# Attention 0 of a two-layer adaLN kernel: side operations two slots apart, a gated output projection in token-major form, and five elementwise steps moved to GpSimd

## The reference

```
mod = (silu(L0_c) @ L0_wmod).reshape(16, 6, 1, 128);  sa, ca, ga = mod[:, 0], mod[:, 1], mod[:, 2]
ga = sign(ga) * max(|ga|, 0.25)
h = layernorm(x) * (1 + ca) + sa
q = h @ Wq + bq;  latent = h @ Wl + bl;  k = latent @ Wk + bk;  v = latent @ Wv + bv     # 16 heads of 8
out = softmax(q k^T / sqrt(8)) v
x = x + ga * (out @ Wo + bo)
```

## Time and profile before

| | us |
|---|---|
| median of three runs | 950.3 |
| lowest and highest | 946.4, 954.19 |
| the profiled execution, its own time | 953.58 |
| its span, first to last instruction | 951.8 |
| attention 0 within the span | about 21 to 348 |

### The profile page before, as it was taken

How to read it: one execution, slowest core, us unless ns; L and a number is a source line. 1 busy time by engine, 2 the same in 40 slices (tenths; PEclk the granted TensorE clock), 3 DMA queues, 4 the chain that set the end, 5 groups by cost and what they waited for, 6 DMA issues and landing times. The chain is left out here.

```text
span 951.8 us, 18404 instructions
## 1 busy us (share of the span) xinstructions
PE 775.1 (81%) x6066; PEld 577.7 (61%) x6066; DVE 677.0 (71%) x1680; ACT 604.3 (63%) x1365; POOL 283.5 (30%) x359
## 2 busy tenths in 40 slices
PE   3458888888688864799999993799988884999996
PEld 3213444444344343799999992678777763888884
DVE  3165777778478627577777654789999964898885
ACT  0214777777477745688888873467877762556553
POOL 3441223242221000000000002234544431767674
PEclk9999999999799976899999996799999995999998
DMA  4353443425953000000000000000000051346340
GB/s 130 41 57 40 56 48 50 54 44 57 171 93 48 4 1 2 1 1 1 1 1 1 2 1 1 1 1 2 2 1 2 1 142 42 89 112 180 107 111 23
DMA packets 76159, 41.04 MB, mean 43 GB/s; under 512 B 6712, under 2 KB 74144, under 8 KB 76064
## 3 DMA queue, kind: packets, MB, share of 16 engines
q1 hardware_dynamic: 76064, 39.83, 22.5%
HBM read 24.62 MB, written 2.23 MB: 28 GB/s over the span
## 5 line engine op out<-in xcount | busy, mean ns | idle before, releaser
L563 DVE TENSOR_REDUCE att_negmax<-att_p_max 128x2 f32<-128x512 f32 x256 | 165.0, 686 | 87.5 <-PE att_p_max L443 86.4
L647 ACT ACTIVATE att_probs<-att_p_sT 128x1024 f32<-128x1024 f32 x128 | 129.6, 1022 | 58.6 <-PE att_p_sT L449 57.6
L443 PE MATMUL att_p_max<-att0p_QK 48*128 48x256 bf16 x512 | 93.8, 295 | 35.9 <-DVE att_negmax L563 11.7
L2050 POOL TENSOR_TENSOR moe_z_lo<-moe_z,moe_z_hi 128x512 fp32r<-128x512 f32 x64 | 96.8, 1528 | 58.2 <-ACT moe_z_hi L2003 56.4
L449 PE MATMUL att_p_sT<-att0p_QK 51*128 51x256 bf16 x512 | 87.6, 284 | 1.2 <-DMA att0p_QK<-att_maxT 1.2
L443 PEld LDWEIGHTS att_p_max<-att0p_QK 48*128 48x128 bf16 x512 | 34.1, 98 | 86.8 <-DVE att_negmax L563 46.2
L928 PE MATMUL ffn0s_p_h<-ffn0s_u_hi,ffn_h_hi 128*128 128x256 f32 x256 | 69.3, 306 | 13.6 <-DVE ffn0s_u_lo L1193 13.0
L472 PE MATMUL att_p_o<-att_probs,att0p_V 128*32 128x256 f32 x1024 | 72.0, 401 | 8.9 <-ACT att_probs L647 7.8
L2041 DVE TENSOR_TENSOR moe_z<-moe_act_u,top_raw 128x512 f32<-128x512 f32 x64 | 73.6, 1150 | 2.2
L1193 DVE TENSOR_TENSOR ffn0s_g_lo<-ffn0s_g,ffn0s_g_hi 128x512 fp32r<-128x512 f32 x64 | 43.3, 691 | 38.8 <-ACT ffn0s_g_hi L1138 37.3
L1134 ACT ACTIVATE ffn0s_g<-ffn0s_p_h,top_ffn_scales 128x256 f32<-128x256 f32 x128 | 54.9, 489 | 19.5 <-PE ffn0s_p_h L929 19.3
(11 more groups left out here) (289 smaller groups left out, 2295.0 us busy)
## 6 DMA issues: line engine op xcount, KB each, us to landing
top_raw<-combine SPq DMA_DIRECT2D x32, 512.0 KB, 6.6
att0p_QK<-att_parts SPq DMA_DIRECT2D x192, 64.0 KB
top_X<-in_L_attn_x SPq DMA_DIRECT2D x4, 512.0 KB, 7.0
top_raw<-in_L_ffn_h_w SPq DMA_DIRECT2D x2, 1024.0 KB
out_x<-top_X SPq DMA_DIRECT2D x8, 256.0 KB, 2.3
prep_wmod<-in_L_wmod SPq DMA_DIRECT2D x2, 384.0 KB, 3.5
top_raw<-in_L_ffn_w_w SPq DMA_DIRECT2D x3, 256.0 KB
att0p_QK<-att_maxT SPq DMA_DIRECT2D x32, 12.0 KB
```

What stands on the lines that cost most here:

```text
L443: mm = pe.matmul(p_max[u % 2][:, i, :], QK[r][rows, g, 0, i * P:(i + 1) * P], QK[r][rows, g, 1, :], start=True, stop=True)
L563: dve.tensor_reduce(negmax[:, :, w, g], p_max[u % 2][:], AX.X, ALU.max, negate=True).then_inc(maxed, 1)
L647: act.activation(probs[g % 2][:, t % 2], p_sT[t % 2][:], ACT.Exp).then_inc(exped, 1)
L2050: pool.tensor_tensor(z_lo[e % RING][:], z[e % RING][:], z_hi[e % RING][:].bitcast(F32), ALU.subtract).then_inc(z_lo_ready, 1)
```

## The change

In `attention0`:

- The side operations of TensorE stand at even slots only, two apart: out 0, ln 2, max_turn 4, O0 6, qk 8, v 10, O1 12, back 14. Each now stands ahead of its slot's tiles.
- The scores of a batch begin at slot 8 of step n-3, not at slot 6 (`SHIFT`). pv stands behind the tiles of slots 14, 0, 4 and 8, not of 11, 15, 3 and 7.
- The projection is token-major: `OTn` is the stationary operand, and the moving one is a copy of Wo whose columns are already multiplied by the gate of that batch. The gated bias is added by a second matmul with one row of ones. `act_y`, `pe_turn_y` and their buffer are gone. The projection and the addition to x move to slot 0 of the next step, so the pipeline is one step longer (21 steps).
- The gated copies of Wo (`wo0_all`, 16 x 128x128) need the gates along the free axis. They are written element by element to DRAM (128x16 values) and read back broadcast to all partitions (1 MB), on SyncE, ahead of the first stack. GpSimd multiplies them by Wo, one batch a step (`pool_wo`).
- Part 0 of the q and k split and the four operations on the maxima move to GpSimd. `negmax` has two buffers. In a step GpSimd now does maxima, parts, layer norm, gated Wo in this order; before it was layer norm, parts.
- VectorE's layer-norm statistics move from slot 2 to slots 8 and 10.

```diff
+SHIFT = 8
+PES = {"out": 0, "ln": 2, "max_turn": 4, "O0": 6, "qk": 8, "v": 10, "O1": 12, "back": 14}
+PV_AT = {14: (3, 0), 0: (4, 1), 4: (4, 2), 8: (4, 3)}
+DVE = {"add": 0, "O0": 6, "stats": 8, "aggr": 10, "O1": 12}
+ACTS = {"hT": 2, "maxT": 4, "qk": 8, "v": 10, "OTn": 14}
+OT_AT = {0: 0, 2: 1, 6: 2, 10: 3}
...
         def pe_out(pe, b):
             pe.wait_ge(OTn_ready, b + 1)
-            pe.matmul(p_m[:, 0:S], k.wo0[:], OTn[:], start=True, stop=True).then_inc(y_made, 1)
+            pe.wait_ge(wo_ready, b + 1)
             for i in range(NT):
+                out = p_m[:, i * D:(i + 1) * D]
+                pe.matmul(out, OTn[:, i * P:(i + 1) * P], k.wo0_all[:, b, :], start=True, stop=False)
+                mm = pe.matmul(out, k.ones_row[0:1, :], k.gbo0_row[0:1, b, :], start=False, stop=True)
+            mm.then_inc(y_made, 1)
...
         def act_qk(act, b, r):
...
-            act.wait_ge(qk_ready, b + 1)
-            at_least(act, stacked, 16 * STACK_DMAS * (b - 1))
-            act.activation(parts[r % 2][:, :, 0], qk[:], ACT.Copy).then_inc(part0_ready, 1)
...
         def pool_parts(pool, b, r):
+            pool.wait_ge(qk_ready, b + 1)
+            at_least(pool, stacked, 16 * STACK_DMAS * (b - 1))
+            pool.tensor_copy(parts[r % 2][:, :, 0], qk[:]).then_inc(part0_ready, 1)
...
+        def pool_wo(pool, b):
+            if b == 0:
+                pool.wait_ge(k.ga0_loaded, 16)
+            pool.tensor_tensor(k.gbo0_row[:, b, :], k.wo0_all[0:1, b, :], k.bo0_row[:], ALU.mult).then_inc(gbo_ready, 1)
+            pool.wait_ge(gbo_ready, b + 1)
+            pool.tensor_tensor(k.wo0_all[:, b, :], k.wo0_all[:, b, :], k.wo0[:], ALU.mult).then_inc(wo_ready, 1)
...
         def pool_step(pool, n, r):
+            if batch_valid(n - 3):
+                pool_negmax(pool, n - 3)
+            if batch_valid(n):
+                pool_parts(pool, n, r)
             if batch_valid(n + 1):
                 pool_normalise(pool, n + 1)
-            pool_parts(pool, n, r)
+            if batch_valid(n - 2):
+                pool_wo(pool, n - 2)
...
-        LAST = B + 4
+        LAST = B + 5
...
         @block.sync
         def _(sp):
+            sp.dma_start(k.ga0_dram.rearrange("b d -> d b"), k.mod[:, 0, GA, :], allow_slow_non_contiguous=True
+                         ).then_inc(k.ga0_stored, 16)
+            sp.wait_ge(k.ga0_stored, 16)
+            sp.dma_start(k.wo0_all[:], k.ga0_dram.rearrange("(o b) d -> o b d", o=1).to_broadcast([P, B, D])
+                         ).then_inc(k.ga0_loaded, 16)
```

More of the change, by code:

```diff
@@ L42 @@
 SROWS = MAXROW + 3
-PES = {"ln": 0, "max_turn": 2, "qk": 3, "O0": 5, "v": 8, "O1": 9, "back": 11, "out": 12, "turn_y": 14,
-       "pv_s": (11, 15), "pv_t": (3, 7)}
-DVE = {"negmax": 0, "stats": 2, "O0": 6, "O1": 10, "add": 15}
-ACTS = {"hT": 0, "maxT": 1, "qk": 3, "v": 7, "OTn": 11, "y": 12, "OT_s": (11, 15), "OT_t": (3, 6)}
+SHIFT = 8
[4 more added lines that the diff above has]
+OT_AT = {0: 0, 2: 1, 6: 2, 10: 3}
 F = 512
@@ L345, in attention0 @@
         parts = [sb(f"parts{n}", [P, 2, 3, S], BF16) for n in range(2)]
-        negmax = sb("negmax", [P, NT, 2, PAIRS])
+        negmax = [sb(f"negmax{n}", [P, NT, 2, PAIRS]) for n in range(2)]
         negrest = sb("negrest", [P, NT, 2, PAIRS])
@@ L455, in pe_max_turn @@
             pe.wait_ge(neg_ready, b + 1)
[L456 to L459 removed]
+            if b + 3 < B:
+                pe.wait_ge(hT_ready, b + 4)
+            at_least(pe, x_added, b - 1)
             for i in range(NT):
@@ L509, in pe_step @@
                     pe_max_turn(pe, s)
+                if slot == PES["O0"] and batch_valid(t):
+                    pe_turn_O(pe, t, 0)
                 if slot == PES["qk"] and batch_valid(f):
@@ L599, in dve_step @@
         def dve_step(dve, n, r):
-            f, m, s, t = n, n - 2, n - 3, n - 4
+            f, m, s, t, y = n, n - 2, n - 3, n - 4, n - 5
             for slot in range(TILES):
-                if slot == DVE["negmax"] and batch_valid(s):
-                    dve_negmax(dve, s)
+                if slot == DVE["add"] and batch_valid(y):
+                    dve_add(dve, y)
                 if slot == DVE["O0"] and batch_valid(t):
@@ L657, in act_OTn @@
             act.activation(OTn[:], p_m[:, 0:S], ACT.Copy).then_inc(OTn_ready, 1)
-        def act_y(act, b):
-            act.wait_ge(y_made, b + 1)
-            at_least(act, y_turned, b)
-            act.activation(yT[:], p_m[:, 0:S], ACT.Identity, bias=k.gbo0[:, bass.ds(b, 1)],
-                           scale=k.mod[:, 0, GA, bass.ds(b, 1)]).then_inc(yT_ready, 1)
         def act_step(act, n, r):
             f, m, s, t = n, n - 2, n - 3, n - 4
-            for slot in range(TILES):
+            for slot in range(0, TILES, 2):
+                if slot in OT_AT and batch_valid(t):
+                    act_OT(act, t, OT_AT[slot])
                 if slot == ACTS["hT"] and batch_valid(f):
@@ L781, in _ @@
                     pool_step(pool, turn * NB + (WHOLE.start + r), r)
-            for n in range(WHOLE.stop, B):
+            for n in range(WHOLE.stop, B + 3):
                 pool_step(pool, n, n % NB)
```

139 lines of the change are left out of this document (62 added, 77 removed).

## The result

The changed kernel takes **991.6 us** (median of four runs, 983.7 to 995.75), the kernel before on the same chip 952.2 (946.4 to 954.19): a ratio of 1.0414, 95% interval 1.033 to 1.0499. It is slower by 4%. The forecast, 961, was slower by 1%, with a chance of 0.43 for more than 1% slower and 0.46 for equal within 1%; the measured time lies above the range, which ended at 973.

What follows compares the result with a forecast made beforehand. No engine is full; the chain of handovers between three engines sets the step. Whole steps -2, stacks +2, gates +5, late loads +2, end +5 sum to +12 on 953.6, moved onto the median: 961 us, range 942 to 973.

Steps and rivals of the forecast that it cites:

- the chain: Handovers between engines from pv group 0 to the next, said to set the whole step: 16.5 us against 16.67.
- the late loads: Step 13, maxima behind four weight loads: loads issued 4.8 us into the step, maxima needed 6.0 later, was 8.1; +2 us.
- One sign: Expected in the trace of whole steps: in each, pv group 1 waiting for the copy to OT0.
- The end: Steps 16 to 18 and the extra step, by the chain walk less 5%: +5 us, bounds +1 and +8.
- The projection: Token-major projection on TensorE beside the chain after pv group 0: eight instructions at v's rate, 1.28 us, ready at 2.84.
- the other branch: Exponential 3, then the copy to OT0 and its handover: lets pv group 1 start 2.82 us behind group 0.
- The whole steps: Whole steps 16.5 us against 16.67, nearly nothing: -2 us over 12 steps, bounds -6 to +6.
- the stacks: Stack DMAs ahead of the next maxima: need 18.4 us, have 17.6; 0.15 a step, +2 us, bounds 0 and +5.
- The gates: Gates' store and 1 MB load ahead of the first stack on SyncE: it lands 0 to 9 us later; +5 taken.
- A: Rival: chain looser than walked, whole step about 15.4 us, 945 us in all, or 938; chance 0.22.
- B: Rival: stack misses slot 8 every step, TensorE waits 0.8 us there, steps of 17.4, 970 us; chance 0.2.

Runs made afterwards that it cites:

- Experiment 1: Changed kernel with the four groups of products with V behind the odd tile, one tile later: 956.2 us, ratio 1.0003 to the kernel before.
- experiment 4: Changed kernel with four more score products, read by nobody, in every slot of steps 18 and 19: 980.3 us, ratio 1.0252 to the kernel before.
- experiment 2: Changed kernel without the ones-row product that adds the gated bias: 977.8 us, ratio 1.0192 to the kernel before.
- experiment 9: Changed kernel with products with V behind the odd tile and without the ones-row bias product: 950.8 us, ratio 0.9951 to the kernel before.
- experiment 10: Kernel before with only the moves to GpSimd (part 0 of the split, four operations on the maxima): 948.9 us, ratio 0.9956.
- experiment 3: Changed kernel with the gates' store behind stack 0 and their load behind stack 1: 988.4 us, ratio 1.0326 to the kernel before.

## Why the prediction was wrong

**What was right.** The prediction named the products with V ahead of the odd tile as what costs, and walked the chain: it gave gaps of 2.82, 4.18, 4.08 and 5.42 between the groups, and the trace has 3.32, 4.18, 4.18 and 5.41. It said that the maxima turn would wait for the layer-norm scale (it stood for 0.75 and started at 161.22; that scale ended at 161.12, GpSimd's last part of the maxima at 158.01), that GpSimd would not be full (7.5 us of 17.08) nor be waited for, and +2 for the late loads (+2.2). Experiment 1 shows that the place of the products is the cause of nearly the whole loss. One sign did not hold: group 1 waited for the projection, 3.32 behind group 0, and not for the copy to OT0.

**The end, +5 and bounds of +1 to +8: the step that failed.** It measured +21.7, and this term alone puts the time above the range. The term priced every product at the full clock and added to before's four intervals what the walk of the chain gave, which makes 14.9, 14.8, 14.3 and 12.2. Measured were 19.25, 15.97, 18.85 and 18.90. The 16.8 that it is short have four parts. The clock: in steps 18 and 19 TensorE's products are on the chain and run at 1.2 GHz, and the two steps pay 6.8 for it, as experiment 4 shows. The walk itself: with the clock held up these two are 16.69 and 14.29, so it was short by 2.4 and 2.1. Step 16, 4.4 over, where TensorE waited 2.62 for the DMA of the turned maxima behind four late loads and its clock fell to 0.66 at 320 to 325 us; how those 4.4 divide was not measured. In experiment 2 the same step had a wait of 1.23 there, kept the full clock and took 15.96. The last 1.2 are in step 17. Nothing in the argument had asked what thinner work does to the clock, though the trace before already shows 0.70 at 345 to 350 us. With the products one tile later the four intervals are 56.8, next to the 56.2 of the forecast; that is luck, since the term was walked for a schedule that this kernel does not have. Its scaling is also a little off: 5% off 15.4 and 15.0 are 14.6 and 14.3, where it took 14.8 and 14.3.

**The projection, 1.28 of TensorE.** It measured 1.66 (155.92 to 157.58). The term priced its eight instructions as v's four, 0.16 each, and they take 0.21. The projection was called an equal of the other branch at 2.84, so its 0.4 over went straight to the step. Experiment 2 took the ones rows out and got 0.40 a step.

**The whole steps, -2, and the stacks, +2.** Together 0 was forecast and +4.1 came. Against the forecast, which had the place of the products in it, the bias product is all of it: without it the step is 16.68. The forecast counted 12 whole steps where there are ten, which is 0.3 us of its sum. The stacks cost nothing in the changed kernel's whole steps, where no wait stands at slot 8; the wait appears when the step is shorter (experiments 1, 9). So +2 was too much here, and it hid part of the miss.

**The gates, +5.** +2.8, within a scatter of 4. The parts were off in opposite senses. Alone, the 2064 packets took 9.3% of 16 engines for 10 us, 7 ns each and not 44 to 70, and had moved by 23.3 us; but the landing was seen at 31.7, at the late end of the 28 to 32 that the term gave. By the Trainium skill's rule (DMA: Bandwidth & Descriptors, Specifications), that transfers under 512 bytes are read, modified and written back, the term should have been nearer +7; no slower packet is to be seen in this store. The DMA view of 21 to 31 us of the changed kernel:

```profile
q1 hardware_dynamic: 2064, 0.01, 9.3%
...
gates<-top_mod SPq DMA_DIRECT2D x1, 8.0 KB, 10.9
```

**The rivals.** A's step of 15.4 is nearly what the changed kernel does with the products one tile later, but in every second step only (15.56), and even then the time only equals that of before, since start, late loads and end give the gain back. A's sum was also off: by the prediction's own terms the others are +14 and not +10, so 949 and not 945. B's wait at slot 8 exists and was hidden. No run takes the two slots and the gated projection apart, so what each of them does alone stays open.

**Where the change's gain went.** Of its three ideas, the moves to GpSimd bring 0.64 a step and 0.44% alone. Two slots and the gated projection together, with the products in the better place, bring 0.1 to 0.2 a step more (15.93 on average over ten whole steps in experiment 1 against 16.13 in experiment 10) and lose more than that at the end (56.8 against 51.25) and at the start.

## What to carry to other kernels

Where two engines hand work to and fro over two buffers, first fix on which side of the buffer's last write the consumer stands: one tile was 35 us here and 102 in the tighter schedule. Judge a step by its chain, but judge a pipeline's end by the clock too: in this kernel's it cost 6.8 us on top of the waits. And look at an engine's copies by what stands behind them: a copy of 0.54 us stood ahead of an exponential that TensorE waited for, and the run that took it away (with four small operations of VectorE) gained 0.64 in each step.

## What the runs showed of the hardware

- A store of 2048 single float32 values to DRAM (8 KB) moved its packets in 1.5 us when alone but landed 10.9 to 11.2 us after its issue. Beside a stack in transfer it landed after 14.8 (14.6 in experiment 3), and the stack itself landed 4.8 us late (49.1 against 44.4). The view of that stretch (79.2% of 16 engines for 11 us) less 427 stack packets at 70 ns leaves some 52 ns for each small packet, an estimate, against 7 alone.
- A float32 product whose contraction has one row took as long as one with 128 when the two alternate, 0.41 and 0.42 us. A projection of two such products with 128 rows took 0.65 us alone and 1.66 with the two one-row products between.
- Four products more a slot, with no reader, made steps 18 and 19 shorter by 6.8 us: the granted clock was 1.00 (2.4 GHz) where it had been 0.50 (1.2 GHz).
- A low clock came in whole steps too: 0.91 on average in the step of 18.11 of experiment 9, behind a wait of 1.73 us, and in the one of 18.20 of experiment 2; the steps right behind them took 14.94 and 16.68.
- The same instructions before the first maxima gave 74.2 and 77.9 us in two runs, and the same code behind attention 0 took 604 to 611.
